# The down product of a mixture of experts in three rounded passes, weights held still, experts weighted by rows

## What is computed

```
x2  = layernorm(x1)                                  # 512 rows of 128
h_e = silu(x2 @ w_gate[e]) * (x2 @ w_up[e])          # 8 experts, F = 512
mix = weights of the 8 experts for each row           # two softmaxes, product, normalised
out = x1 + sum over e of mix[:, e] * (h_e @ w_down[e])
```

## Time and profile before

| | |
|---|---|
| median of three runs | 1698.93 us (1697.87 to 1699.07) |
| profiled execution, own time | 1692.36 us |
| its span, first to last instruction | 1690.5 us |
| mean granted TensorE clock | 0.981 |
| TensorE busy | 1560.0 us (92%) |
| VectorE busy | 1025.8 us (61%) |
| ScalarE busy | 949.1 us (56%) |
| GpSimd busy | 410.8 us (24%) |
| DMA queue of SyncE | 8.7% of the 16 engines' span |

### The profile page before, as it was taken

How to read it: one execution, slowest core, us unless ns; L and a number is a source line. 1 busy time by engine, 2 the same in 40 slices (tenths; PEclk the granted TensorE clock), 3 DMA queues, 4 the chain that set the end, 5 groups by cost and what they waited for, 6 DMA issues and landing times. The chain is left out here.

```text
span 1690.5 us, 31436 instructions
## 1 busy us (share of the span) xinstructions
PE 1560.0 (92%) x12484; PEld 1305.2 (77%) x12484; DVE 1025.8 (61%) x2316; ACT 949.1 (56%) x1302; POOL 410.8 (24%) x403
## 2 busy tenths in 40 slices
PE   5389978999999899998999999989999999999998
PEld 2278866888778787787878778777788888888887
DVE  5556656765766567666665576556755675476543
ACT  5273737753686456836666486356743665276421
POOL 5332331422213222124211241113411221022000
PEclk9999989999999999999999999999999999999999
DMA  5010110002000200010001200021001000100000
GB/s 180 13 38 26 60 55 10 34 10 57 2 22 31 58 12 2 29 53 34 8 1 36 77 3 8 1 74 41 1 1 51 7 1 2 51 2 8 1 7 7
DMA packets 39426, 47.11 MB, mean 28 GB/s; under 512 B 5120, under 2 KB 21504, under 8 KB 39280
## 3 DMA queue, kind: packets, MB, share of 16 engines
q1 hardware_dynamic: 39280, 45.10, 8.7%
HBM read 25.97 MB, written 2.33 MB: 17 GB/s over the span
## 5 line engine op out<-in xcount | busy, mean ns | idle before, releaser
L948 ACT ACTIVATE h<-pg 128x512 f32<-128x512 f32 x512 | 304.5, 598 | 609.5 <-PE pg L261 607.0
L892 PE MATMUL pd<-w_down,h 128*128 128x128 f32 x4096 | 544.3, 282 | 0.6 <-DVE x L974 0.6
L892 PEld LDWEIGHTS pd<-w_down,h 128*128 128x128 f32 x4096 | 511.3, 195 | 31.5 <-issue 9.0
L994 DVE TENSOR_TENSOR h<-h,pu 128x512 f32<-128x512 f32 x512 | 347.2, 680 | 187.4 <-PE pu L261 185.9
L799 POOL TENSOR_TENSOR att_arena<-att_arena 100x500 f32<-100x500 f32 (+2 forms) x192 | 172.9, 900 | 613.5 <-DVE att_arena L741 605.8
L259 PE MATMUL pg<-ffn_x_hi,w_gate_hi 128*128 128x512 f32 x512 | 247.7, 484 | 0.0
L259 PE MATMUL pu<-ffn_x_hi,w_up_hi 128*128 128x512 f32 x512 | 205.7, 402 | 9.5 <-DVE h L994 9.5
L260 PE MATMUL pg<-ffn_x_lo,w_gate_hi 128*128 128x512 f32 x512 | 205.6, 402 | 0.0
L261 PE MATMUL pg<-ffn_x_hi,w_gate_lo 128*128 128x512 f32 x512 | 205.1, 401 | 0.0
L260 PE MATMUL pu<-ffn_x_lo,w_up_hi 128*128 128x512 f32 x512 | 205.0, 400 | 0.0
L261 PE MATMUL pu<-ffn_x_hi,w_up_lo 128*128 128x512 f32 x512 | 204.7, 400 | 0.0
(11 more groups left out here) (170 smaller groups left out, 1778.5 us busy)
## 6 DMA issues: line engine op xcount, KB each, us to landing
arena<-bc_spread SPq DMA_DIRECT2D x56, 256.0 KB
q<-qk_parts SPq DMA_DIRECT2D x128, 64.0 KB, 2.1
k<-qk_parts SPq DMA_DIRECT2D x128, 64.0 KB, 2.1
arena<-in_x SPq DMA_DIRECT2D x8, 256.0 KB, 2.8
x<-in_x SPq DMA_DIRECT2D x8, 256.0 KB, 3.3
h<-in_w_gate SPq DMA_DIRECT2D x8, 256.0 KB, 6.5
h<-in_w_up SPq DMA_DIRECT2D x8, 256.0 KB, 2.8
w_down<-in_w_down SPq DMA_DIRECT2D x8, 256.0 KB, 4.3
```

What stands on the lines that cost most here:

```text
L892: last = nc.tensor.matmul(pd[:, t * P:(t + 1) * P], h_b[:, d % NH, t * P:(t + 1) * P], wd[:, d % NCH, :], start=d % CPE == 0 and t == 0, s ...
L948: nc.scalar.activation(h_b[:, c % NH, :], pg[c % 2][:, :], ACT.Silu).then_inc(gate_done, 1)
L994: nc.vector.tensor_tensor(h, h, pu[d % 2][:, :], ALU.mult).then_inc(h_done, 1)
```

## The change

The down product is turned round. `w_down` becomes the weights and `h` what streams, so `pd` comes out as 128 features by 512 rows, in three rounded passes by `split3`. For that `w_down` is split once into hi and lo (8 pieces, `split_wd` on ScalarE and GpSimd), and every chunk of `h` too: ScalarE copies it rounded into `h_hi` (a ring of 4), and the rest `h_lo` is taken by GpSimd for two chunks in three and by VectorE for the third (`on_pool`). `LAG` is 5, the ring of `h` has 7 buffers.

As rows now lie along the free axis, the weight of an expert is a row: TensorE transposes `mix` (4 small transposes), ScalarE copies it, SyncE writes it to memory, and reads for each expert one row spread over 128 partitions (`mix_row`, 128 DMAs in all). VectorE multiplies `pd` by it (one 128x512 instead of four 128x128), and GpSimd adds the experts up (`ffn_sum`, 112 additions). After the eighth expert TensorE transposes the sum back (`back`, 4 transposes), and VectorE adds it to `x`. The routing logits are taken in three rounded passes as well, which drops a float32 copy on ScalarE. The table of V for attention is packed tighter (16 small copies for each attention in place of 4), and some due times are shifted.

```diff
-LAG = 4
+LAG = 5
-NH = 8
+NH, NHI = 7, 4
+T_BACK = [NCH * (m + 1) + LAG + 2 for m in range(NM)]
+T_END = [t + 1.5 for t in T_BACK]
-T_ATT = [38 + 55 * b for b in range(B)]
-ATT_PACE = [2.6] + [3.0] * (B - 2) + [2.5]
+T_ATT = [42] + [38 + 55 * b for b in range(1, B - 1)] + [425.5]
+ATT_PACE = [2.3] + [3.0] * (B - 2) + [2.3]
+        def on_pool(d):
+            return d % 3 != 2
 # Head.pe
-                    last = nc.tensor.matmul(ps[:, t * 2 * E:(t + 1) * 2 * E], fx[slot][:, t * P:(t + 1) * P],
-                                            pk("w_route"), start=True, stop=True)
+                    nc.tensor.matmul(out, xh, wr[0][:, :], start=True, stop=False)
+                    nc.tensor.matmul(out, xl, wr[0][:, :], start=False, stop=False)
+                    last = nc.tensor.matmul(out, xh, wr[1][:, :], start=False, stop=True)
+                yield t0 + 8.5
+                for t in range(TT):
+                    last = nc.tensor.transpose(ps[0:E, t * P:(t + 1) * P], mix[:, t, :], ident)
+                yield T_BACK[m]
+                pe.wait_ge(added, adds(E * (m + 1)))
+                for t in range(TT):
+                    last = nc.tensor.transpose(ps[:, t * P:(t + 1) * P], acc[:, t * P:(t + 1) * P], ident)
 # Head.sp, new
+                sp.dma_start(mix_r, mix_t).then_inc(mix_out, 16)
+                for e in range(E):
+                    n = E * m + e
+                    yield max(T_HEAD[m] + 9.5, NCH * m + CPE * e + LAG + (CPE - 8))
+                    if n >= 2:
+                        if (n - 2) % E:
+                            sp.wait_ge(added, adds(n - 1))
+                        else:
+                            sp.wait_ge(weighed, n - 1)
+                    sp.dma_start(mrow[n % 2][:, :], mix_r[e:e + 1, :].broadcast_to([P, L])).then_inc(mix_in[n % 2], 16)
 # TensorE, chunk(c)
                     for d in downs(c):
-                        pe.wait_ge(h_done, d + 1)
-                        if d % CPE == 0 and d:
-                            pe.wait_ge(summed, TT * (d // CPE))
-                        for t in range(TT):
-                            last = nc.tensor.matmul(pd[:, t * P:(t + 1) * P], h_b[:, d % NH, t * P:(t + 1) * P],
-                                                    wd[:, d % NCH, :], start=d % CPE == 0 and t == 0,
-                                                    stop=d % CPE == CPE - 1 and t == TT - 1)
-                        last.then_inc(down_done, 1)
+                        if on_pool(d):
+                            pe.wait_ge(lo_done, pool_los(d) + 1)
+                        else:
+                            pe.wait_ge(lo_dve, d - pool_los(d) + 1)
+                        if d % CPE == 0:
+                            if d:
+                                pe.wait_ge(weighed, d // CPE)
+                        split3(pd[:, :], [w[:, d % NCH, :] for w in wd], (hh_b[:, d % NHI, :], hl_b[:, d % NH, :]),
+                               d % CPE == 0, d % CPE == CPE - 1).then_inc(down_done, 1)
 # ScalarE, chunk(c), behind silu
+                    d = c - 3
+                    if 0 <= d < NC:
+                        act.wait_ge(h_done, d + 1)
+                        if d >= NHI:
+                            act.wait_ge(down_done, d - NHI + 1)
+                        nc.scalar.copy(hh_b[:, d % NHI, :], h_b[:, d % NH, :]).then_inc(hi_done, 1)
 # VectorE, weigh(e) and chunk(c)
+                    dve.wait_ge(mix_in[e % 2], 16 * (e // 2 + 1))
                     dve.wait_ge(down_done, CPE * (e + 1))
-                    for t in range(TT):
-                        nc.vector.scalar_tensor_tensor(x[:, t, :], pd[:, t * P:(t + 1) * P],
+                    nc.vector.tensor_tensor(m[:, :] if e % E else acc[:, :], pd[:, :], m[:, :], ALU.mult).then_inc(weighed, 1)
+                    d = c - 4
+                    if 0 <= d < NC and not on_pool(d):
+                        dve.wait_ge(hi_done, d + 1)
+                        nc.vector.tensor_tensor(hl_b[:, d % NH, :], h_b[:, d % NH, :], hh_b[:, d % NHI, :].bitcast(F32),
+                                                ALU.subtract).then_inc(lo_dve, 1)
 # GpSimd, chunk(c)
+                    d = c - 4
+                    if 0 <= d < NC and on_pool(d):
+                        pool.wait_ge(hi_done, d + 1)
+                        nc.gpsimd.tensor_tensor(hl_b[:, d % NH, :], h_b[:, d % NH, :], hh_b[:, d % NHI, :].bitcast(F32),
+                                                ALU.subtract).then_inc(lo_done, 1)
+                    e, last = divmod(c - 1 - LAG, CPE)
+                    if e >= 0 and last == CPE - 1 and e % E:
+                        pool.wait_ge(weighed, e + 1)
+                        nc.gpsimd.tensor_tensor(acc[:, :], acc[:, :], mrow[e % 2][:, :], ALU.add).then_inc(added, 1)
```

More of the change, by code:

```diff
@@ L37 @@
 NXB = 4
-NH = 8
+NH, NHI = 7, 4
 T_HEAD = [-9, 25] + [NCH * m - 8 for m in range(2, NM)]
-T_END = [NCH * (m + 1) + LAG + 1.5 for m in range(NM)]
+T_BACK = [NCH * (m + 1) + LAG + 2 for m in range(NM)]
+T_END = [t + 1.5 for t in T_BACK]
 def _ssm_slots(i):
@@ L101, in build @@
         wu = [sb(f"w_up_{v}", [P, NCH, P], F32R) for v in ("hi", "lo")]
-        wd = sb("w_down", [P, NCH, P])
+        with contextlib.ExitStack() as shared:
+            wd_raw = shared.enter_context(nc.sbuf_tensor("w_down", [P, NCH, P], F32))
+        wd = [sb(f"w_down_{v}", [P, NCH, P], F32R) for v in ("lo", "hi")][::-1]
+        wr = [sb(f"w_route_{v}", [P, 2 * E], F32R) for v in ("hi", "lo")]
         wq = [sb(f"w_q_{v}", [P, P], F32R) for v in ("hi", "lo")]
@@ L113, in build @@
         xn_ffn = sb("ffn_rows", [P, TT, D])
-        fx = [sb(f"ffn_x{s}", [P, L]) for s in range(2)]
         fxh = [sb(f"ffn_x_hi{s}", [P, L], F32R) for s in range(2)]
         fxl = [sb(f"ffn_x_lo{s}", [P, L], F32R) for s in range(2)]
-        h_b = sb("h", [P, NH, L])
-        u_b = sb("staged", [P, 3, L])
+        with contextlib.ExitStack() as shared:
+            h_b = shared.enter_context(nc.sbuf_tensor("h", [P, NH, L], F32))
+        hl_b = sb("h_lo", [P, NH, L], F32R)
+        with contextlib.ExitStack() as shared:
+            u_b = shared.enter_context(nc.sbuf_tensor("staged", [P, 3, L], F32))
+        hh_b = sb("h_hi", [P, NHI, L], F32R)
+        acc = sb("ffn_sum", [P, L])
+        mrow = [sb(f"mix_row{s}", [P, L]) for s in range(2)]
+        mix_d = [nc.dram_tensor(f"mix_bc_spread{s}", (E, L), F32, kind="Internal").ap() for s in range(2)]
         ln_buf = {k: (sb(f"bn6_{k}", [P, TT, 6]), sb(f"mv_{k}", [P, TT, 2]), sb(f"rstd_{k}", [P, TT]))
@@ L125, in build @@
         lmax = sb("route_max", [P, TT, 2])
-        mix = [sb(f"mix{s}", [P, TT, E]) for s in range(2)]
+        mix = sb("mix", [P, TT, E])
+        mix_t = xn_ffn[0:E, :, :].rearrange("p t d -> p (t d)")
         cws = sb("mix_sums", [P, TT, 4])
@@ L131, in build @@
         btile, ctile = ([arena[:, i + s, :] for s in range(2)] for i in (6, 8))
-        bc_t = sb("bc_rows", [2 * DSTATE, L])
+        bc_rows = [(xn_ffn[:, :, :].rearrange("p t d -> p (t d)") if i == 0 else tot)[0:2 * DSTATE, :] for i in range(B)]
         bc_d = [nc.dram_tensor(f"bc_spread{s}", (2 * DSTATE, L), F32, kind="Internal").ap() for s in range(2)]
@@ L261, in split3, with adds, pool_los @@
             return nc.tensor.matmul(out, w[1], x_parts[0], start=False, stop=last)
+        def adds(e):
+            return (E - 1) * (e // E) + max(e % E - 1, 0)
+        def on_pool(d):
+            return d % 3 != 2
+        def pool_los(d):
+            return sum(on_pool(i) for i in range(d))
         def tok(rows_d, i):
@@ L326, in act @@
                 nc.scalar.activation(lg[:, :, 1, :], lg[:, :, 1, :], ACT.Exp, scale=10.0).then_inc(route_exp, 1)
+                yield t0 + 9
+                b.wait(act, ("mix", m))
+                b.free(nc.scalar.copy(mix_t, b.ps(("mix", m))[0:E, :]), ("mix", m))
             @staticmethod
@@ L356, in dve @@
                                         ALU.mult).then_inc(mix_ready, 1)
+                yield T_BACK[m] + 1
+                b.wait(dve, ("back", m))
+                x = rows(xb[ORDER[m][0] % NXB])
+                b.free(nc.vector.tensor_tensor(x, b.ps(("back", m))[:, :], x, ALU.add), ("back", m))
+                b.wait_free(dve, ("back", m))
             @staticmethod
@@ L955, in small_weights, with split_wd @@
                     nc.scalar.activation(neg_a[:, :], neg_a[:, :], ACT.Ln, bias=1.0).then_inc(w_prep, 1)
-                interleave([(small_weights, 0)] + [(Ssm.act, i) for i in range(B)] + [(Att.act, j) for j in range(B)]
+                def split_wd(act, link, e):
+                    yield CPE * e - 3
+                    act.wait_ge(wd_loaded[e], 16)
+                    nc.scalar.copy(wd[0][:, CPE * e:CPE * (e + 1), :],
+                                   wd_raw[:, CPE * e:CPE * (e + 1), :]).then_inc(wd_hi, 1)
```

(1 more changed line is left out.)

115 lines of the change are left out of this document (75 added, 40 removed).

## The result

The kernel became slower: 1768.97 us, the median of four runs, against 1698.4 us of the kernel before (with a fourth run beside the three of the table above), a ratio of 1.0424 (95% interval 1.0388 to 1.0459). The prediction of 1678 us was wrong in its direction, and the result lies beyond the end of its range (1738). Its profiled execution took 1772.81 us with a span of 1771.0 us, 80.5 us above that of the earlier trace rows.

The account below looks back on a forecast made before the run. TensorE was taken as the bound (busy 1560.0 of 1690.5 us). -58 + 12 + 26 + 10 + 5 = -5 us, with a third off the stalls -21: span 1670, profiled 1672, forecast 1678 us; range 1640 to 1738.

Parts of the forecast that it names:

- I cost it at nothing: VectorE's added and dropped instructions (-89, +116, +11, +20 or so us): engine stays near 65% busy, so no cost.
- rival 2: Whole kernel slower through GpSimd's order and the shared port: 175 us more on VectorE, 1723 us; chance 0.29.
- rival 2's 450 instructions: VectorE instructions using SBUF alone (scans, factors, layer norms, new subtractions), each held up 0.39 us on average by GpSimd.
- one of its two signs: In the changed profile: waits on h_lo spread over all attention units, or VectorE's two-operand instructions grown by 0.4 us.
- GpSimd's order, +26: TensorE's down products wait behind GpSimd's ordered work, mainly in the ssm stretches: +26 us, 10 to 60.
- ScalarE, +12: 512 rounded copies fill ScalarE in its fullest stretches, delaying the copies of P: +12 us, 0 to 39.
- TensorE, -58: TensorE's own work: -95 us from rounded down products, +15 for switches, +22 for transposes and logits, net -58 us.
- the 15 us: In attention the float32 switch moves ahead of the down product: 190 times 0.08 us, 15 us come back on TensorE.
- The granted clock: TensorE's clock falling below 0.981 in new idle times was named as a sign of being wrong, without a price.
- SyncE, +10: The mix rows queue among SyncE's DMAs, so TensorE's waits for k get longer: +10 us, 0 to 20.
- end and setup, +5: After the last up product: copy, subtraction, additions and transposes, less a weigh step and shorter products: +5 us.
- A third off: Stalls across engines overlap, so a third is taken off their 48 us, moving the sum from -5 to -21 us.

Follow-up runs that it names:

- kernel 9: The change with all subtractions still made, but TensorE not waiting for them (it streams h_hi in the second pass): 1766.2 us, 1.0412 of the kernel before.
- kernel 11: The change with only GpSimd's 342 subtractions made, VectorE's 170 left out, and TensorE waiting for none: 1724.49 us, 1.0182 of the kernel before.
- kernel 1: The change without the 512 subtractions for h_lo; the second pass streams h_hi instead: 1676.28 us, 0.9904 of the kernel before.
- kernel 2: The change without the 512 subtractions and without ScalarE's 512 rounded copies; VectorE writes its product rounded: 1634.99 us, 0.9657 of the kernel before.
- kernel 4: The kernel before with ScalarE's 512 new copies added on a buffer nobody reads or waits for: 1721.86 us, ratio 1.0179.
- kernel 3: The kernel before with 454 GpSimd subtractions added on a buffer nobody reads or waits for: 1726.93 us, ratio 1.0207.
- 12: The kernel before with both idle loads added, GpSimd's 454 subtractions and ScalarE's 512 copies: 1745.0 us, ratio 1.0312.
- kernel 5: The kernel before with GpSimd's added load made of memsets of 128x1500, which write but read nothing: 1714.26 us, ratio 1.0119.

## Why the prediction was wrong, step by step

**The step that failed: VectorE, "I cost it at nothing".** It counted VectorE's new and dropped instructions at their undisturbed lengths, which gives +58 us of work, gave this no price, and left the lengthening of all others to rival 2. The lengthening is in the trace (387 to 881, 856 to 1413, 1296 to 1543 ns) and the runs show its consequence: removing only the wait for `h_lo` gives nothing (kernel 9), removing VectorE's subtractions 39 us (kernel 11), and removing GpSimd's as well another 47 (kernel 1), of the 88 in all. The row that could have told it stood in the prediction: 1.27 us beside GpSimd, 0.68 alone. It was used for a rival and given no term in the sum. The layer norms, 128 tensor_scalars in groups of four most of them with TensorE's transposes right behind, were counted among rival 2's 450 instructions, but nothing was said of TensorE waiting for them. These waits went from 4.8 to 21.3 us for the experts' rows.

**Rival 2** had the direction and, for VectorE, the mechanism and one of its two signs: of the two-operand instructions the factor grew by 0.56 us, the scan by 0.25. Its 175 us more on VectorE were some 140 (the 78% that it made of them should have been 75: 65% and 175 of some 1680 us). The other sign, waits on `h_lo` spread over all attention units, was not met. There are 17 such waits, 13 of them in or right behind a stretch of the ssm on GpSimd, where the forecast had put them. Its 1723 us was 46 too low. It had no term for ScalarE (+42) and none for the clock; how the 46 us split was not tested.

**GpSimd's order, +26.** As a wait on TensorE it came out in size and place: 24.9 us on `h_lo`. As a term it is wrong, since without the wait the time stays the same (kernel 9). Other waits grow when these 24.9 us go.

**ScalarE, +12.** Mis-sized: 42 us by kernels 1 and 2, 30 by kernel 4. The place was right (the copies of P in attention); its stated upper end of 39 was the better value. The 18 us of kernels 1 and 2 are the longer wait on these copies alone.

**TensorE, -58.** Mis-sized to the other side. Per plain chunk 0.24 us is saved (9.19 less 8.24, by four), not 95/512 = 0.185. The switch behind the product was already in the 0.89 us of the earlier trace rows. What was not foreseen is that all nine passes of a chunk now start 0.229 us apart, where the six of gate and up took 0.234 and the prediction 0.235, and no run shows why. In eight steps of an attention without other waits (chunks 240 to 248) 1.7 us are saved (25.0 to 23.3 us, 0.21 a chunk), 0.2 less than in plain chunks. The switch does stand ahead of the new product there (0.34 us to its second pass at 940.44), as predicted, but less came back in these steps than the 0.4 us that the 15 us mean for them. 512 times 0.22 or so is 113, less some 20 for transposes and logits: about -93, an estimate. Kernel 2, with a clock of 0.968, has TensorE 81.2 us less busy and 25 us more idle. That its time comes out 58 us below the kernel before, the very number of this term, is a coincidence.

**The granted clock** had no term at all. It was named as a sign, not as a price. Between kernel 2 and the change it is some 31 of the 51.1 us by which the same matmuls are busy for longer (an estimate, above).

**SyncE, +10, and end and setup, +5:** near enough. The wait for k went from 28.0 to 33.7 in the changed kernel, and to 40.0 in kernel 2, where less else is waited for. The end runs 17.7 us behind the last gate pass where it was 12.6, and the first gate pass starts 2.4 us later. The pieces listed for the end sum to 4.3 us before anything is taken off, so its +5 was a little more than its own working gives. Three rows of it (timeline of the changed kernel) carry the waits that were foreseen:

```profile
1758.31 0.47 PE L289 MATMUL pd<-h_hi,w_down_hi 128*128 128x512 f32 x1 [1.45 <-DVE mix_row L1072]
1760.82 0.50 PE L289 MATMUL pd<-h_hi,w_down_hi 128*128 128x512 f32 x1 [0.88 <-POOL h_lo L1154]
...
1765.31 1.09 PE L366 MATMUL side_ps<-pack,ffn_sum 128*128 128x128 f32 x4 [2.28 <-POOL ffn_sum L1162]
```

**"A third off":** of the right kind; a fifth where it was tried (kernels 3, 4 and 12).

What stays open: how much of the 47 us that GpSimd's subtractions cost is the port and how much is its place in the order, for which ssm and attention on VectorE wait. Without GpSimd's reads kernel 5 is 15 us better than kernel 3, but its memsets are longer and hold up the layer norms more, so it bounds neither part. Nor was a version run in which the layer norms avoid tensor_scalar.

## What to carry to other kernels

Before giving GpSimd a steady load, list VectorE's instructions that share its port (two inputs from SBUF, and tensor_scalar on SBUF), multiply their number by GpSimd's busy share and by half the length of one of its instructions, and put that in the sum as a term, above all where TensorE waits right behind them. Here that working, rival 2's, gave 175 us of VectorE's time, and some 140 came. What of it reaches the kernel's time has to be measured. A wait in the trace on the new instruction is not its price: test it by making the work and not waiting for it, and by leaving the work out. And this kernel, which lives on TensorE, paid for part of its idle time again in the granted clock, so a saving that leaves the other engines fuller should be discounted by both.

## What the hardware showed that I had not expected

- One 128x128 tensor_scalar of the layer norm took 3.46 us beside three GpSimd instructions that followed on each other, where the mean before was 387 ns. It was not let in between them. On average over 64 it was 881 ns, with a median of 340.
- GpSimd instructions that only write (memsets of 1350 ns) held tensor_scalar up more than ones that read (subtractions of 1061 ns): 1033 against 569 ns. They left the scan and its factor alone (1293 and 852 ns). How much of the difference is the memsets' length was not tested.
- With all 512 on one engine, a subtraction of 128x512 on GpSimd cost this kernel twice what one on VectorE did (0.24 against 0.12 us), with VectorE at 79% in the latter case. Added in two steps, GpSimd's came to 0.14 and VectorE's to 0.23.
- TensorE's clock fell in a kernel whose TensorE is still 86% busy: 0.981 to 0.948, with seven of the 40 slices at 0.8 where one was. The slices of the kernel before:

```profile
PEclk9999989999999999999999999999999999999999
```

A window of the change between 450 and 500 us, columns as in the earlier trace rows:

```profile
450.00:500.00 50.00, 45.30 (x308) 35.38 (x307) 29.74 (x53) 31.71 (x48) 22.91 (x21) 0.93 0.20 60
```

There TensorE is busy for as long as in that window before (45.30 against 45.40 us), at 0.93 of full speed instead of 0.97; the work in the two windows is not the same.
